# A linear-attention and MLP layer on one core: first loads in pieces, VectorE's queue reordered, and seven matmuls on a cleared tile

## The reference

```python
x = x + attn(layernorm(x))
x = x + ffn(layernorm(x))

# attn: 16 heads of 32, chunks of 128 tokens, state S per head
q, k = rotate(silu(x @ Wq)), rotate(silu(x @ Wk))
v = x @ Wv
scores = (q_i @ k_i^T) * D                 # D: decay mask within the chunk
o = scores @ v_i + (q_i * decay_q) @ S
S = lam^128 * S + (k_i * decay_k)^T @ v_i
o = group_rmsnorm(o * sigmoid(x @ Wg1 @ Wg2)) * norm_weight
return o @ Wo

# ffn: weights of 4 bits with a scale per block of 32, MLP width 4096
return (gelu(x @ Wgate^T) * (x @ Wup^T)) @ Wdown^T
```

## Time and profile before

| | |
|---|---|
| median of 3 runs | 1421.55 us (1420.71 to 1422.2) |
| the profiled execution | 1420.75 us |
| its span | 1418.7 us |
| TensorE busy | 1361.8 us (96%) |
| VectorE busy | 1048.3 us (74%) |
| ScalarE busy | 419.1 us (30%) |
| GpSimd busy | 246.6 us (17%) |
| DMA | 40.20 MB, 28 GB/s over the span |

### The profile page before, as it was taken

How to read it: one execution, slowest core, us unless ns; L and a number is a source line. 1 busy time by engine, 2 the same in 40 slices (tenths; PEclk the granted TensorE clock), 3 DMA queues, 4 the chain that set the end, 5 groups by cost and what they waited for, 6 DMA issues and landing times.

```text
span 1418.7 us, 18934 instructions
## 1 busy us (share of the span) xinstructions
PE 1361.8 (96%) x7120; PEld 1126.0 (79%) x7120; DVE 1048.3 (74%) x1682; ACT 419.1 (30%) x666; POOL 246.6 (17%) x137
## 2 busy tenths in 40 slices
PE   5789999997999999999999999999999999999998
PEld 3677778786778888888888888888888888888886
DVE  6878787777776868677776868686777768686844
ACT  4333343332322323222222222222223222232221
POOL 3424433343110111010110101110101101010100
PEclk9999999998999999999999999999999999999999
DMA  9000000000000100000000000000000000000002
GB/s 325 10 16 1 2 15 0 15 1 1 1 30 15 34 27 30 16 30 15 30 30 15 30 15 30 27 32 15 30 15 30 28 16 30 15 30 16 1 30 89
DMA packets 21740, 40.20 MB, mean 28 GB/s; under 512 B 2624, under 2 KB 2880, under 8 KB 21568
## 3 DMA queue, kind: packets, MB, share of 16 engines
q1 hardware_dynamic: 21696, 39.60, 8.4%
HBM read 35.40 MB, written 4.19 MB: 28 GB/s over the span
## 4 chain that ended last, share of the span: by engine, by line
PE 86%; DVE 7%; issue 3%; POOL 2%; ACT 1%; DMA 1%; SPq 0%; DVEq 0%; POOLq 0%; ACTq 0%
PE bank L878 27%; PE bank L879 27%; PE bank L880 27%; PE bank L890 1%; PE bank L959 1%; PE bank L976 1%; POOL rb L796 1%; PE bank L1064 1%; POOL qr L804 1%; DMA w_in<-wv_dram 1%; PE bank L966 1%; DVE x1l L706 0%; DVE nt_t L482 0%; DVE nt_t L484 0%; DVE qa L526 0%
## 5 line engine op out<-in xcount | busy, mean ns | idle before, releaser
L878 PE MATMUL bank<-x1h,wh 128*128 128x512 f32 x1024 | 398.5, 389 | 0.0
L880 PE MATMUL bank<-x1h,wl 128*128 128x512 f32 x1024 | 398.4, 389 | 0.0
L879 PE MATMUL bank<-x1l,wh 128*128 128x512 f32 x1024 | 398.4, 389 | 0.0
L816 POOL TENSOR_TENSOR wl<-wf,wh 128x1024 fp32r<-128x1024 f32 (+1 forms) x48 | 114.9, 2394 | 896.5 <-ACT wh L361 896.5
L878 PEld LDWEIGHTS bank<-x1h,wh 128*128 128x128 f32 x1024 | 192.2, 188 | 40.0
L880 PEld LDWEIGHTS bank<-x1h,wl 128*128 128x128 f32 x1024 | 192.2, 188 | 39.9
L879 PEld LDWEIGHTS bank<-x1l,wh 128*128 128x128 f32 x1024 | 192.2, 188 | 39.8
L878 PE MATMUL bank<-wh,hh 128*128 128x512 f32 x512 | 200.1, 391 | 3.2 <-DVE x1l L706 3.2
L743 DVE SCALAR_TENSOR_TENSOR hx<-hx,bank 128x512 f32<-128x512 f32 x128 | 88.0, 687 | 154.4 <-ACT hx L439 154.4
L880 PE MATMUL bank<-wh,hl 128*128 128x512 f32 x512 | 199.7, 390 | 0.0
L879 PE MATMUL bank<-wl,hh 128*128 128x512 f32 x512 | 199.7, 390 | 0.0
(11 more groups left out here) (108 smaller groups left out, 1481.8 us busy)
## 6 DMA issues: line engine op xcount, KB each, us to landing
pk<-packed_dram SPq DMA_DIRECT2D x48, 256.0 KB
sc<-scales_dram SPq DMA_DIRECT2D x48, 256.0 KB
acc<-x_dram SPq DMA_DIRECT2D x4, 1024.0 KB, 12.6
out_dram<-acc SPq DMA_DIRECT2D x16, 256.0 KB, 2.2
w_in<-wq_dram SPq DMA_DIRECT2D x1, 1024.0 KB, 7.2
w_in<-wk_dram SPq DMA_DIRECT2D x1, 1024.0 KB, 9.7
w_in<-wv_dram SPq DMA_DIRECT2D x1, 1024.0 KB, 9.0
maskT<-mask_dram SPq DMA_DIRECT2D x1, 1024.0 KB, 10.3
```

The source lines that it names most:

```text
L816: nc.gpsimd.tensor_tensor(wl[par][:, bass.ds(u, 1), :].rearrange("p a w -> p (a w)"), wf[:].rearrange("p a w -> p (a w)"), wh[par][:, bass ...
L878: pe.matmul(dst, w_h, x_h, start=start, stop=False)
L879: pe.matmul(dst, w_h, x_l, start=False, stop=False)
L880: return pe.matmul(dst, w_l, x_h, start=False, stop=stop)
```

## The change

- **Loads.** The first chunk of x is loaded by itself, with a semaphore of its own, then Wq and Wk in halves, then the other three chunks of sequence 0, then Wv in halves, the tables, x of sequence 1, Wo, and x of sequences 2 and 3. The identity, both gate weights (the second in one DMA, not four), the rotation table and the norm weight are issued by ScalarE.
- **Prologue.** Statistics are made for chunk 0 alone, later for chunks 1 to 3. High and low parts of Wq, Wk and Wv are made in halves, and the first q, k and v products wait for them by halves.
- **Wo.** The scaling by the norm weight is no longer a pass of its own: ScalarE's cast (`wo_hi`) and VectorE's subtraction (`wo_lo`, behind chunk 0) multiply by it, in four pieces each.
- **Chunks.** On VectorE the gating stands ahead of the state's update. `unit_bits` is cut in two: two instructions go behind `decayed_q` of chunk 2, three ahead of its gating; `unit_scale` goes to chunk 3, ahead of the gating. Statistics of x of sequences 2 and 3 are made together behind chunk 0. On GpSimd `kd` stands behind the state's scaling, and `unit_lo` moves from chunk 3 to behind chunk 0 of the next sequence, as does `unit_hi` on ScalarE.
- **Matmuls on a cleared tile.** The state `st` is cleared first of all, and TensorE multiplies it by itself (float32, 128x128 by 128x512), five times ahead of the first transposes and twice behind them. The results, in bank 7, are overwritten unread.

```diff
             def load_w(n, slot):
-                sp.dma_start(w_in[:, slot, :].rearrange("p (k n) -> p k n", k=KT),
-                             w_view[n]).then_inc(s_w[n], 16)
...
-            load_x(0)
-            sp.dma_start(idt[:], ident).then_inc(s_id, 16)
+                for h in range(2):
+                    sp.dma_start(w_in[:, slot, 1024 * h:1024 * h + 1024]
+                                 .rearrange("p (k n) -> p k n", k=2),
+                                 w_view[n][:, 2 * h:2 * h + 2, :]).then_inc(s_w[n][h], 16)
+
+            sp.dma_start(acc[:, 0:1, :], xv[:, 0:1, :]).then_inc(s_xt0, 16)
             load_w(0, 0)
             load_w(1, 1)
-            sp.dma_start(g1_in, wg1.rearrange("(k p) n -> p k n", p=P)).then_inc(s_small, 16)
-            for r in range(4):
-                sp.dma_start(g2_in[32 * r:32 * r + 32, :], wg2).then_inc(s_small, 16)
+            sp.dma_start(acc[:, 1:CHUNKS, :], xv[:, 1:CHUNKS, :]).then_inc(s_x[0], 16)
             load_w(2, 2)
-            sp.dma_start(rotT[:], rot).then_inc(s_tab, 16)
-            sp.dma_start(maskT[:], mask.rearrange("p r g t -> p r (g t)")).then_inc(s_tab, 16)
             sp.dma_start(dqT[:], decay_q).then_inc(s_tab, 16)
             sp.dma_start(dkT[:], decay_k).then_inc(s_tab, 16)
             sp.dma_start(lamT[:], lam_c).then_inc(s_tab, 16)
-            for b in range(1, BATCH):
+            sp.dma_start(maskT[:], mask.rearrange("p r g t -> p r (g t)")).then_inc(s_tab, 16)
+            load_x(1)
+            sp.wait_ge(s_whi, 2)
+            sp.wait_ge(s_wlo, 2)
+            load_w(3, 0)
+            for b in range(2, BATCH):
                 load_x(b)
-            sp.dma_start(nw[:], norm_w).then_inc(s_nw, 16)
-            sp.wait_ge(s_whi, 1)
-            sp.wait_ge(s_wlo, 1)
-            load_w(3, 0)
@@ -298,10 +297,25 @@
...
-            def weight_hi(n, slot):
-                act.wait_ge(s_w[n], 16)
-                A(w_hi[n][:], w_in[:, slot, :].rearrange("p (k n) -> p k n", k=KT),
+            act.dma_start(idt[:], ident).then_inc(s_id, 16)
+            act.dma_start(g1_in, wg1.rearrange("(k p) n -> p k n", p=P)).then_inc(s_small, 16)
+            act.dma_start(g2_in, wg2.unsqueeze(0).broadcast_to([4, HD, 512])).then_inc(s_small, 16)
+            act.dma_start(rotT[:], rot).then_inc(s_rot, 16)
+            act.dma_start(nw[:], norm_w).then_inc(s_nw, 16)
+
+            def weight_hi(n, slot, h):
+                act.wait_ge(s_w[n][h], 16)
+                A(w_hi[n][:, 2 * h:2 * h + 2, :],
+                  w_in[:, slot, 1024 * h:1024 * h + 1024].rearrange("p (k n) -> p k n", k=2),
                   ACT.Copy).then_inc(s_whi, 1)
+
+            def wo_hi():
+                act.wait_ge(s_nw, 16)
+                for h in range(2):
+                    act.wait_ge(s_w[3][h], 16)
+                for k in range(KT):
+                    A(w_hi[3][:, k, :], w_in[:, 0, 512 * k:512 * k + 512], ACT.Copy,
+                      scale=nw[:, k:k + 1]).then_inc(s_whi, 1)
@@ -361,26 +375,24 @@
...
-            weight_hi(0, 0)
+            weight_hi(0, 0, 0)
             norm1(0, 1)
-            weight_hi(1, 1)
+            weight_hi(0, 0, 1)
             xt_hi_(0)
-            weight_hi(2, 2)
-            norm1(1, 1)
-            act.wait_ge(s_small, 16 * 5)
+            weight_hi(1, 1, 0)
+            weight_hi(1, 1, 1)
+            act.wait_ge(s_small, 16 * 2)
             A(g1s[:], g1_in.unsqueeze(2).broadcast_to([P, KT, 4, HD]), ACT.Copy).then_inc(s_ghi, 1)
-            for r in range(4):
-                A(g2s[32 * r:32 * r + 32, :], g2_in[32 * r:32 * r + 32, :],
-                  ACT.Copy).then_inc(s_ghi, 1)
+            A(g2s[:], g2_in, ACT.Copy).then_inc(s_ghi, 1)
+            weight_hi(2, 2, 0)
+            weight_hi(2, 2, 1)
             tanh_qk(0)
             gate_low(0)
+            norm1(1, 2)
             v_copy(0, 0)
             xt_hi_(1)
-            norm1(2, 1)
+            norm1(2, 2)
             tanh_gate(0)
-            act.wait_ge(s_wob, 1)
-            A(w_hi[3][:], w_in[:, 0, :].rearrange("p (k n) -> p k n", k=KT),
-              ACT.Copy).then_inc(s_whi, 1)
@@ -400,11 +412,13 @@
...
                     ahead = (c + 3) // CHUNKS + 1
-                    norm1(t + 3, b + ahead)
-                if c == 3 and not near_end(b, c, 1):
-                    unit_hi(b, b, 0)
+                    norm1(t + 3, b + ahead + 1)
+                if at_start(b, c):
+                    wo_hi()
                 ot_copy(t)
                 square(t)
+                if c == 0 and not (isinstance(b, int) and b == 0):
+                    unit_hi(b - 1, b - 1, 0)
@@ -486,27 +500,39 @@
...
+            def weight_lo(n, slot, h):
+                dve.wait_ge(s_whi, 2 * n + h + 1)
+                V.tensor_tensor(w_lo[n][:, 2 * h:2 * h + 2, :],
+                                w_in[:, slot, 1024 * h:1024 * h + 1024]
+                                .rearrange("p (k n) -> p k n", k=2),
+                                w_hi[n][:, 2 * h:2 * h + 2, :].bitcast(F32),
+                                ALU.subtract).then_inc(s_wlo, 1)
...
+            def wo_lo():
+                dve.wait_ge(s_nw, 16)
+                for k in range(KT):
+                    dve.wait_ge(s_whi, 6 + k + 1)
+                    V.scalar_tensor_tensor(out=w_lo[3][:, k, :],
+                                           in0=w_in[:, 0, 512 * k:512 * k + 512],
+                                           scalar=nw[:, k:k + 1], in1=w_hi[3][:, k, :].bitcast(F32),
+                                           op0=ALU.mult, op1=ALU.subtract).then_inc(s_wlo, 1)
             def xt_lo_(t):
@@ -615,32 +647,32 @@
...
-            stats(0)
-            stats_r(0)
+            V.memset(st[:], 0.0).then_inc(s_st0, 1)
+            dve.wait_ge(s_xt0, 16)
+            stats(0, 1)
+            stats_r(0, 1, 0)
+            weight_lo(0, 0, 0)
+            xt_lo_(0)
             weight_lo(0, 0, 1)
-            xt_lo_(0)
-            weight_lo(1, 1, 2)
-            dve.wait_ge(s_ghi, 5)
+            weight_lo(1, 1, 0)
+            weight_lo(1, 1, 1)
+            dve.wait_ge(s_ghi, 2)
             V.tensor_tensor(g1s[:, :, 2, :], g1_in, g1s[:, :, 2, :].bitcast(F32),
                             ALU.subtract).then_inc(s_glo, 1)
             V.tensor_tensor(g2s[32:64, :], g2_in[32:64, :], g2s[32:64, :].bitcast(F32),
                             ALU.subtract).then_inc(s_glo, 1)
-            V.memset(st[:], 0.0).then_inc(s_st0, 1)
+            dve.wait_ge(s_x[0], 16)
+            stats(1, CHUNKS)
+            stats_r(1, CHUNKS, 1)
             silu_qk(0)
             gate_low(0)
-            dve.wait_ge(s_tab, 16 * 5)
+            dve.wait_ge(s_rot, 16)
             rope_of(None, 0, 0, 0)
             xt_lo_(1)
-
-            dve.wait_ge(s_w[3], 16)
-            dve.wait_ge(s_nw, 16)
-            for k in range(KT):
-                ins = V.tensor_scalar(w_in[:, 0, 512 * k:512 * k + 512],
-                                      w_in[:, 0, 512 * k:512 * k + 512], nw[:, k:k + 1], None,
-                                      ALU.mult)
-            ins.then_inc(s_wob, 1)
-            stats(1)
-            stats_r(1)
+            dve.wait_ge(s_x[1], 16)
+            stats(CHUNKS, 2 * CHUNKS)
+            stats_r(CHUNKS, 2 * CHUNKS, 2)
+            dve.wait_ge(s_tab, 16 * 4)
@@ -660,19 +692,24 @@
                 if not at_start(b, c):
                     normed(t - 1)
                 decayed_q(t)
+                if c == 2 and not near_end(b, c, 4):
+                    unit_bits_a(b, b, [32] * UNITS)
                 if not near_end(b, c, 1):
                     silu_qk(t + 1)
                     gate_low(t + 1)
                     rope_of(b, c, t + 1, (c + 1) % CHUNKS)
                 if not at_start(b, c):
                     ot_lo_(t - 1)
-                else:
-                    weight_lo(3, 0, 4)
...
                     add_x1(t - 1)
+                if c == 2 and not near_end(b, c, 4):
+                    unit_bits_b(b, b)
+                if c == 3 and not near_end(b, c, 4):
+                    unit_scale(b, b)
+                gated(t)
@@ -687,16 +724,14 @@
...
                     ins.then_inc(st_done, 1)
-                gated(t)
                 if isinstance(b, int) and b == 0:
-                    if c in (0, 3):
-                        stats({0: 2, 3: 3}[c])
-                    if c in (1, 3):
-                        stats_r({1: 2, 3: 3}[c])
-                if c == 1 and not near_end(b, c, 4):
-                    unit_bits(b, b, [32] * UNITS)
-                if c == 2 and not near_end(b, c, 4):
-                    unit_scale(b, b)
+                    if c == 0:
+                        wo_lo()
+                        dve.wait_ge(s_x[2], 16)
+                        dve.wait_ge(s_x[3], 16)
+                        stats(2 * CHUNKS, TILES)
+                    if c == 1:
+                        stats_r(2 * CHUNKS, TILES, 3)
@@ -819,24 +854,25 @@
...
```

(41 more changed lines are left out.)

44 lines of the change are left out of this document (23 added, 21 removed).

## The result

| | before | after |
|---|---|---|
| median (runs beside each other) | 1421.27 us (4) | 1411.15 us (4) |
| range of the runs | 1420.71 to 1422.2 | 1410.31 to 1411.68 |
| the profiled execution | 1420.75 us | 1411.68 us |
| its span | 1418.7 us | 1409.8 us |

The ratio is 0.9928, with a 95% interval of 0.991 to 0.9945: 10 us faster, where 18.6 were forecast.

What follows compares the result with a forecast made beforehand. TensorE's idle time and low clock in the first 350 us were taken as what can be won; 3.3 (lead) + 11.9 (waits) + 3.4 (clock) = 18.6 off 1420.75 gave 1402.2, median 1403.0, range 1397 to 1411 us.

Steps and rivals of the forecast that it cites:

- 11.9 of waits: TensorE's waits between 60 and 330 us: of 15.8 us, 11.9 won by reordering the chunks, 2.2 and 1.7 left or new.
- 3.4 of clock: Granted clock after idle: with the waits gone, 2.4 us back in 80:100 and 1.0 in batch 3.
- Rival (e): Chunks 2 and 3: bits and `unit_scale` ahead of gating make `normed` late; slower than before, 1433 us; chance 0.03.
- The lead at chunk 1's scores: Chunk 1's scores at 58.6 against 64.33, 5.5 us ahead; 3.3 left after low clock and late `otl` take 2.2.
- Wv's second half lands where Wv landed (the same bytes are ahead of it), 15.8: Start: Wv's second half lands at 15.8 us, on the way to chunk 1 starting at 24.6 against 30.27.
- I cost that at nothing: Loads: five move to ScalarE's queue, idle until Wq's first half near 6 us; claimed cost nothing.
- Rival (c): Start: first pieces share engines with ScalarE's loads, land 1.5 to 2 us later; some 3 of 5.7 left; 1406; chance 0.08.
- Aggregation and Newton (2.7): VectorE's chain in the start, for chunks 1 to 3: these steps take 2.7 us; the chain ends at 23.4.
- With less time at the low clock 4.7: Behind chunk 0's `intra`: statistics begin 4.7 us after it instead of 5.5, at 45.2.
- rival (a): Chunk 1's new stall is worse (dear w_lo, slowed BN_STATS, low clock until 70): 3.3 becomes -1 to -2; 1408; chance 0.2.
- 19.3 less 3.36 for chunk 1's start to `intra`: Chunk 0: without w_lo for Wo this stretch takes 15.9 us, so `intra` is at 40.5, 9.0 ahead.
- three signs of being wrong: Transposes start after 9.5 us, products run at 0.42 all through 60:70, or TensorE waits for `normed` in every batch.

## Why the prediction was half right

**Direction and main source: right.** The chunk reorder won most of what was forecast. From chunk 1's scores to the end 13.4 us were gained (4.5 behind turned into 8.9 ahead, by the profiled executions), where 11.9 of waits and 3.4 of clock, 15.3, stood in the sum; the reorder alone gave 12.5. By the earlier trace rows and the waits above, the waits gave some 9.3 and not 11.9, so some 4 are clock and last chunks. Of the waits I left 3.9; 6.5 stayed, since `otl` behind the rotation still comes late in sequences 0 and 3. Rival (e), slower by late gating, had no support anywhere: TensorE never waits for `normed` in chunks 2 and 3 of sequences 0 to 2. The MLP stayed as it was. The sum stopped at 330 and so never had the longest wait of the last chunks, 4.15 us, which the change left at 3.51.

**The lead at chunk 1's scores: wrong, by 10.** Forecast 5.5 us ahead (3.3 after two deductions), measured 4.5 behind. That is 7.8 of the 9.5 us that are missing between the profiled executions (1402.2 forecast, 1411.68 measured); the rest is the 1.9 above. In its steps the scores came at 68.81 instead of 58.6: 6.6 late at chunk 1's start, 1.6 more to `intra`, 1.95 more to the extra tasks, 0.1 behind them.

- "Wv's second half lands where Wv landed (the same bytes are ahead of it), 15.8" **failed first**: it was cast at 20.07. Counting bytes presumes that all bytes move at one rate. "I cost that at nothing" for ScalarE's loads is the same mistake, as "The sum by it is the same, since I let bytes set the landings" was. With the second gate weight in four DMAs the cast is at 16.28, close to the forecast. This took 2.65 us of the time. My edit list named that DMA ("the second in one DMA, not four") and gave it no price. Rival (c), at 0.08, had loads in each other's way, but only for the first piece, and by the sharing of engines, not by the shape of one load; x in fact landed earlier than forecast.
- "Aggregation and Newton (2.7)" **failed second**: beside GpSimd's product the steps alone, from 20.75 until silu began at 26.47, took 5.7. Each slow instruction ended just as one half of GpSimd's did. Even with the weights on time chunk 1 starts at 27.37, not 24.6; with Wv's low part on VectorE 1.2 us of that come back.
- "With less time at the low clock 4.7": **failed third**: the extra tasks began 6.65 us behind `intra`; 50:60 ran at 0.75. Statistics (4.84), the low part of Wo (2.74) and the path from the reduction to the scores (6.1, forecast 6.0) were as taken. The stall itself was foreseen (its wait within the 3.5 given back, the clock and `otl` behind it at 2.2), and moving the 2.74 of it gave about 3 us. It looks like rival (a), but that rival's conditions aren't there: Wo's low part wasn't dear, BN_STATS wasn't slowed, and 60:70 ran at 0.93. The time came near its 1408 for other reasons.
- 19.3 less 3.36 for chunk 1's start to `intra`: 17.5 measured, 1.6 over. The products of 30:40 ran at 0.83. That term is in part luck: the same stretch ran at 0.83 and 0.99 in traces of kernels that are alike up to there, and chunk 0's scores of the reorder alone came 2.1 us behind the kernel before with the same code ahead of them. So up to 2 us of the 4.5 behind can be the executions' own.

None of the three signs of being wrong came true (the transposes started at 8.68, not after 9.5; 60:70 was not at the low clock throughout; `normed` was not late in every batch). The miss showed only in the list of places ahead of them: chunk 1 at 31.18 where 24.6 was forecast.

**The matmuls on the cleared tile: right.** They end near 8.8, the transposes start at 8.68 (forecast 8.2), and they bring nothing. That the clock rises is what the Trainium skill says (TensorE: Matmul & The Clock Gate, Part 1: The HAM clock gate); the trace agrees (products 0.42 apart without them, 0.23 with them), but the time doesn't follow, for the reason forecast.

## What to carry to other kernels

Price a load by the shape in which it is cut, too: look for a stretch in which the DMA share is full and the GB/s are low, and cut or move the load that runs there. An extra task goes where its engine idles ahead of a result that comes late anyway, not behind it; here such a move of 2.7 us gave about 3, since the clock held as well. Before crediting a lead to an edit, look whether it stands already ahead of the first instruction that was moved. And follow waits by place, not by a fixed window: as the start moves, a wait slides in or out of it. Warm the clock only if the products that it speeds up end something.
